# Expert stage of a four-stage kernel: activations laid out with the token innermost, down tables loaded during the up takes, output operations split around the layernorm

## What is computed

```python
def kmoe(x_flat, W_router, A, B, scale, bias, d_in1, d_in2, d_out1, d_out2, top_k):
    logits = x_flat @ W_router.T
    vals, idx = jax.lax.top_k(logits, top_k)
    probs = jax.nn.softmax(vals, axis=-1)
    xs = x_flat.reshape(-1, d_in1, d_in2)
    Ag = A[idx]
    Bg = B[idx]
    Y = jnp.einsum('nkoi,nij,nkpj->nkop', Ag, xs, Bg)
    out = jnp.einsum('nkop,nk->nop', Y, probs).reshape(-1, d_out1 * d_out2)
    return out * scale + bias
...
h = kmoe(x_flat, W_up, A_up, B_up, scale_up, bias_up, D1, D2, F1, F2, TOP_K)      # 32x32 -> 64x64, E=64, TOP_K=2
h = jax.nn.gelu(h, approximate=False)
y = kmoe(h, W_down, A_down, B_down, scale_down, bias_down, F1, F2, D1, D2, TOP_K)  # 64x64 -> 32x32
```

## Time and profile before

| | us |
|---|---|
| median of 3 runs | 875.33 |
| lowest and highest of them | 874.97, 879.26 |
| the profiled execution, its own time | 870.78 |
| its span, first to last instruction | 868.8 |
| granted clock, mean over the span | 0.900 |

### The profile page before, as it was taken

The page is one execution under the profiler, slowest core; times in us unless marked ns, Lnnn a source line. Parts: engine busy times, 40 slices in busy tenths (PEclk is TensorE's granted clock), DMA queues, the critical chain, the costliest instruction groups (busy, mean ns, idle before and its releaser), DMA issues. The chain is left out here.

```text
span 868.8 us, 18294 instructions
## 1 busy us (share of the span) xinstructions
PE 654.9 (75%) x7522; PEld 386.0 (44%) x7554; DVE 519.9 (60%) x1094; ACT 344.7 (40%) x522; POOL 358.8 (41%) x330
## 2 busy tenths in 40 slices
PE   0627878788786389868875478248998988999995
PEld 0313444444444389758765324123333344444442
DVE  8656666676664633221502668878999984415265
ACT  1422444334443653330423463246554535434320
POOL 9202444444442300000001062328998983966530
PEclk9968999999998579878868599659999998999999
DMA  3156540000000632200000470000000000000000
GB/s 76 36 120 150 68 66 0 0 0 0 0 1 1 223 85 49 53 3 2 2 5 5 136 235 0 0 0 1 0 1 0 0 1 1 1 0 1 12 13 24
DMA packets 17326, 29.75 MB, mean 34 GB/s; under 512 B 3248, under 2 KB 13168, under 8 KB 16240
## 3 DMA queue, kind: packets, MB, share of 16 engines
q1 hardware_dynamic: 17264, 28.87, 13.1%
HBM read 24.54 MB, written 4.19 MB: 33 GB/s over the span
## 5 line engine op out<-in xcount | busy, mean ns | idle before, releaser
L474 ACT ACTIVATE pr_exp<-at_psum 128x1024 f32<-128x1024 f32 x68 | 69.6, 1024 | 128.2 <-PE at_psum L559 128.2
L366 DVE TENSOR_REDUCE pr_neg_max<-at_psum 128x4 f32<-128x1024 f32 x68 | 83.2, 1225 | 49.7 <-PE at_psum L541 49.7
L316 POOL TENSOR_SCALAR_AFFINE_SELECT pr_exp<-pr_exp 128x512 f32<-128x512 f32 x68 | 47.1, 692 | 155.6 <-ACT pr_exp L474 155.6
L1481 POOL TENSOR_TENSOR all_phi_b<-all_phi_b,mo_work 128x512 f32<-128x512 f32 x56 | 71.0, 1268 | 44.6 <-ACT mo_work L1687 40.0
L749 POOL TENSOR_TENSOR all_x<-all_x,ff_x_blocks 128x512 f32<-128x512 f32 x3 | 3.8, 1267 | 187.5 <-ACT ff_x_blocks L933 187.5
L1502 PE MATMUL all_psum<-all_phi,mo_xt 128*128 128x512 f32 x128 | 66.3, 645 | 7.4 <-ACT mo_work L1669 5.6
L1451 POOL TENSOR_TENSOR mo_work<-mo_work,mo_max 128x1024 f32<-128x1024 f32 x32 | 61.4, 1918 | 21.5 <-DVE mo_max L1743 21.5
L536 PE MATMUL at_psum<-band_mask,all_ident_bf 128*128 128x512 bf16 x104 | 35.7, 401 | 40.9 <-DVE pr_q_window L359 27.6
L1535 PE MATMUL all_psum<-mo_xt,all_phi_centred 128*128 128x512 f32 x128 | 66.3, 598 | 0.0
L1588 PE MATMUL all_psum<-mo_work,mo_y_slots 128*128 128x512 f32 x128 | 62.5, 595 | 1.8 <-DVE mo_work L1791 1.8
L1687 ACT ACTIVATE mo_work<-all_psum 128x512 f32<-128x512 f32 x64 | 37.7, 601 | 61.9 <-PE all_psum L1535 61.9
(11 more groups left out here) (339 smaller groups left out, 1335.6 us busy)
## 6 DMA issues: line engine op xcount, KB each, us to landing
all_expert_w<-in_expert_w SPq DMA_DIRECT2D x1, 4096.0 KB, 18.2
ff_b_up<-in_b_up SPq DMA_DIRECT2D x1, 2048.0 KB, 9.1
ff_a_up<-in_a_up SPq DMA_DIRECT2D x1, 2048.0 KB, 14.0
ff_w_down<-in_w_down SPq DMA_DIRECT2D x2, 1024.0 KB, 20.7
at_q_stack<-parts_scratch SPq DMA_DIRECT2D x24, 64.0 KB
at_k_stack<-parts_scratch SPq DMA_DIRECT2D x24, 64.0 KB
at_q_stack<-parts_scratch SPq DMA_DIRECT2D x12, 128.0 KB
at_k_stack<-parts_scratch SPq DMA_DIRECT2D x12, 128.0 KB
```

The source lines that it names most:

```text
L316: nc.gpsimd.affine_select(out=e[:, g, :, 0, :], in_=e[:, g, :, 0, :], compare_op=ALU.is_ge, fill=0.0, base=0, pattern=[[0, GH], [-1, P]], ...
L366: nc.vector.tensor_reduce(negm[:, GH * g:GH * g + GH].rearrange("p (u r) -> p r u", r=2), psum[:, SN + 2 * (g % 2):SN + 2 * (g % 2) + 2, : ...
L474: nc.scalar.activation(e[:, g, :, :, :].rearrange("p h j q -> p (h j q)"), psum[:, ST:ST + 2, :].rearrange("p b n -> p (b n)"), ACT.Exp).t ...
L1481: nc.gpsimd.tensor_tensor(tot[:, ch % 2, :], first, ec[:, ch % 2, j, :], ALU.add).then_inc(added, 1)
```

## The change

Four edits, all in `kmoe`. One: `h` becomes `[P, F1, N]`, so that one number of all 128 token positions stands side by side and the 64 numbers of a token position stand 512 bytes apart. L815 then writes single numbers 512 bytes apart, L906 works on 32 runs of 32, the down logits' moving operand (`h[rows, o, :]`) is one run, and the weights of `first_down` (`h[rows, :, n]`) are read 512 bytes apart. Two: `z` and `vs` move to `ta`, the down tables to `tb`. Three: SP waits for 16 instead of 32 take units in front of the down tables' four DMAs. Four: `finish` in `norm_y` is split. VectorE does `variance(gr)`, `take_y(gr+1)`, `invert(gr)`; ScalarE does `root_y(0)`, `take_v(6)`, `norm_y(0)`, `take_v(7)`. Line numbers behind L849 move by up to 5.

```diff
-        h = a.sb("h", [P, N, F1])
+        h = a.sb("h", [P, F1, N])
...
-        z = tb_flat.rearrange("p (u g k n) -> p u g k n", u=2, g=16, k=K)
-        vs = tb_flat.rearrange("p (u s n k b) -> p u s n k b", u=4, s=2, n=8, k=K)
-        bdn = ta_flat[:, 0:D1 * F1].rearrange("p (b n) -> p b n", b=D1)
-        adn = ta_flat[:, D1 * F1:].rearrange("p (b n) -> p b n", b=D1)
+        z = ta_flat.rearrange("p (u g k n) -> p u g k n", u=2, g=16, k=K)
+        vs = ta_flat.rearrange("p (u s n k b) -> p u s n k b", u=4, s=2, n=8, k=K)
+        bdn = tb_flat[:, 0:D1 * F1].rearrange("p (b n) -> p b n", b=D1)
+        adn = tb_flat[:, D1 * F1:].rearrange("p (b n) -> p b n", b=D1)
...
-                sp.wait_ge(got, 2 * UB)
+                sp.wait_ge(got, UB)
...
-                        v.scalar_tensor_tensor(out=h[:, 32 * j + r:32 * j + 32:4, :], in0=psum[:, h_bank(4 * j + r), :].rearrange("p (g o) -> p g o", o=F1),
+                        v.scalar_tensor_tensor(out=h[:, :, 32 * j + r:32 * j + 32:4].rearrange("p o g -> p g o"), in0=psum[:, h_bank(4 * j + r), :].rearrange("p (g o) -> p g o", o=F1),
...
-                    ln_y.finish(dve, 4 * gr, 4 * gr + 4, gr)
+                    ln_y.variance(dve, 4 * gr, 4 * gr + 4)
...
                     norm_y(gr)
                     if gr < 3:
                         take_y(gr + 1)
+                    ln_y.invert(dve, 4 * gr, 4 * gr + 4, gr)
...
-                        part = h[:, 32 * j + 16 * k:32 * j + 16 * k + 16, :].rearrange("p n o -> p (n o)")
+                        part = h[:, 32 * k:32 * k + 32, 32 * j:32 * j + 32]
...
+                def root_y(gr):
+                    ln_y.root(act, 4 * gr, 4 * gr + 4, gr)
+
                 def norm_y(gr):
-                    ln_y.root(act, 4 * gr, 4 * gr + 4, gr)
                     act.wait_ge(ln_y.factors, gr + 1)
...
                 for ch in range(6):
                     take_v(ch)
+                root_y(0)
+                take_v(6)
                 norm_y(0)
-                take_v(6)
                 take_v(7)
                 for gr in range(1, 4):
+                    root_y(gr)
                     norm_y(gr)
...
-                        last = t_.matmul(psum[col:col + 64, s, 0:N], wdn[rows, o, :], h[rows, :, o], start=(o < 2), stop=(o >= F1 - 2))
+                        last = t_.matmul(psum[col:col + 64, s, 0:N], wdn[rows, o, :], h[rows, o, :], start=(o < 2), stop=(o >= F1 - 2))
...
-                                last = t_.matmul(psum[64 * w:64 * w + 64, v_bank(ch) + s, 64 * n2:64 * n2 + 64], h[rows, n, :],
+                                last = t_.matmul(psum[64 * w:64 * w + 64, v_bank(ch) + s, 64 * n2:64 * n2 + 64], h[rows, :, n],
```

More of the change, by code:

```diff
@@ L682, in kmoe @@
         ln, ln_y = Norm(nc, a, "ln_x", NT), Norm(nc, a, "ln_y", NT)
-        flat = h[:, :, :].rearrange("p n o -> p (n o)")
+        flat = h[:, :, :].rearrange("p o n -> p (o n)")
         xt = flat[:, 0:T * R]
```

## The result

Measured again side by side, the kernel before takes 877.59 us (median of 7 runs, 874.97 to 881.57) and the changed kernel 868.26 us (median of 7, 865.43 to 872.73). The ratio is 0.9898, with a 95% interval of 0.9867 to 0.9929: 9 us less, 6 to 12. A second comparison of 5 rounds gives 0.9891 [0.9864, 0.9919]. The direction held, and 868.26 lies inside the range of 855 to 870. The size did not hold: the sum promised 15.1 us, and 868.26 is outside the forecast's own 856 to 864, in the part of rival 1.

What follows compares the result with a forecast made beforehand. The prediction took TensorE to bound the down logits, and instruction supply plus take_y waits the down products. Its terms, -9.9 - 3.7 - 1.5 = -15.1 us from 875.33, gave 860.2 us (forecast 856 to 864, range 855 to 870).

Steps and rivals of the forecast that it cites:

- rival 1: Gain partly eaten: first_down at 56 ns a row removes Term C's gain; 865 us, range 864 to 870, chance 0.22.
- Term A: Down logits: with the moving operand as one run they fall from 18.66 to 8.8 us, gain 9.9.
- Term B: Down products: first_down's strided weight loads take 35 ns a row, hidden by the instruction supply; cost 0.
- L815, the term that failed: Writes of single numbers into h: cost taken as 0, upper bound 0.4 us each, 2.5 us on the path.
- Term C: Down products: reordered output operations remove take_y pauses; supply of 3.45 us a block limits the gain to 3.7 us.
- Rival 4: More than forecast: supply not fixed at 3.45 us a block, reordering gives 6.55; 857 us, chance 0.04 (under 856).
- Term D: Up products, second(0): down table loads 14 us earlier no longer delay an instruction block; gain 1.5 us, between 0 and 3.0.
- The tail: End of the down products: VectorE's last adds are untouched and the tail behind 480.7 stays.
- Rivals 2 and 3: First_down's strided loads don't overlap, 893 us, chance 0.11; repeated PSUM adding, not stride, sets logits' pace, 870, chance 0.08.

Runs made afterwards that it cites:

- logits_run: Kernel before, with the down logits' moving operand read as one run of 128 numbers from the old layout (wrong numbers); 864.23 us in one profiled run.
- after_again: The changed kernel measured once more without edit, 5 rounds; 865.17 us against 874.57 for the kernel before, ratio 0.9891.
- weights_run: Changed kernel, with first_down's weights read as one run of 64 numbers (wrong numbers); 864.24 us in one profiled run.
- layout_only: Kernel before with the new layout of h alone; 872.45 us against 876.43, ratio 0.9954.
- packed_tail: Changed kernel, with each h write going to 8 adjacent token positions and the third group's invert back ahead of the last take_y; 861.89 us, ratio 0.9838.
- order_only: Kernel before with only the output operations reordered; 874.27 us against 876.43, ratio 0.9972.
- half_second: Changed kernel, with only the first expert's half of second_down computed, 512 matmuls and 512 weight loads fewer; 850.96 us in one profiled run.
- loads_only: Kernel before with the down tables loaded 14 us earlier and the buffers swapped; 876.35 us against 876.43, ratio 0.9987.
- tail_order: Changed kernel, with only the third group's invert put back ahead of the last take_y; 863.0 us against 878.11, ratio 0.982.

## Why the prediction was right in sign and two thirds in size

First, the level. Side by side, the kernel before has 877.59 us, 2.3 more than the 875.33 that the forecast started from. The same sum from there gives 862.5, so 5.8 of the 8.1 us between 860.2 and 868.26 are errors of the terms and the rest is this shift.

**Term A, right; one number off.** Forecast 18.66 to 8.8, measured 9.95: 8.7 won instead of 9.9. The pace is L1049's in the windows (some 53 and 27 ns when the whole stage is divided at 398.3), and `logits_run` shows that the step alone made it. What was mis-sized is the moment of the clock's rise. I took 395, 4.2 us into the stage (the trace of before has 394.6); in after the granted clock is 0.50 for 5.7 us, until 398.3. Each microsecond at 0.50 instead of 1.00 costs about half a microsecond now that the rows follow the clock, where the strided rows did not care. That moment varies between executions: the ten profiles with one run have 8.70 to 10.11 us, among them 8.70 in `after_again`, where the forecast's 8.8 is met. The 67 and 70 ns of the prediction are windows divided by rows cut by their edges; from start to start both are 71 ns, which makes its reading, one pace at either clock, only firmer.

**Term B, right, with a condition that I saw only in part.** The middle value of 35 ns came out as 35 to 37, and `weights_run` shows the stage no shorter without it, within the 1.4 us that it varies. The prediction costed B as if C were given. `layout_only` has B without C, and there 1.9 us of `first_down`'s slower rows stand in front of the `take_y` pauses: the order of the terms matters. By medians edit one alone gives 4.0 us, edit four 2.2, edits two and three 0.1; together 6.3, against 9.3 for all four. Each of the three has an interval of 2 to 3 us to either side, so all of the 3 us may be chance; that the slower rows are on the path in `layout_only` rests on its rows, not on the medians.

**L815, the term that failed.** I took 0 and a bound of 0.4 us for each write, from TensorE's penalty for a strided number. Measured is 0.35 us each, near the bound. The writes go in pairs, and two of them took 1.41 us before and 2.05 after. At the three places on the path (j = 0, 1 and 3) the rows of after fall behind those of before by 0.60, 0.63 and 0.58 us, some 1.8 us. As a whole time it was not measured by itself, and `packed_tail`, which takes it back, is only 0.4 us shorter than `after_again` in the up stage, as a stretch there ran at half clock. The wrong step was to take runs of 4 numbers, 256 bytes apart, as the nearest row for single ones. The right bound was in hand and was left out of the sum. The Trainium skill, "SBUF — State Buffer", Door 1: The DMA port swizzle, with its 16-byte lines, had spoken against this write: runs of 4 fill such a line, single numbers don't, and the three rows (746 ns for runs of 8, 1122 for steps of 16 bytes, 1100 for 512) agree with it.

**Term C, the mechanism right, the size not.** The pauses went, and the supply was what came next, as the prediction said. It took 3.45 us for a block from one clean step of the earlier trace rows, and so 41.65 us would become 37.95. From fetch to fetch, twelve steps take 43.56 us in after, 3.63 each, 44.75 in `after_again`, 3.73 each, and 46.30 in `packed_tail`, 3.86 each; single ones go up to 4.00 in `order_only` and from 3.35 to 4.13 in `half_second`. So the stage is 1.6 us shorter than before's in after, 0.6 in `order_only`, 0.2 in `after_again` and longer in `packed_tail`: C's size lies between nothing and 1.6 us in these executions, not at 3.7, and it is not firmer known than that. The kernel before had four steps of 3.43 to 3.46 us in a row, where `logits_run`, with the same code in that stretch, has 3.70 to 4.01, and the lowest step of a supply is no mean of it. Rival 4, that the supply gives way and C brings 6.55, is excluded: `order_only` has all `take_y` waits removed and still takes 45.30 us, `weights_run` 44.47. Why one step is 3.4 us and another 4.1 is open; no run changed it by itself. The granted clock does not part them: before has 3.45 at 0.50, and `half_second` has both 3.35 and 4.13 at 1.00. The transfer of a block is not the whole step either: 1.9% of 16 engines over 48 us, for 13 blocks, is 1.1 us each.

**Term D, a wash.** The pause in second(0) fell by 1.3 us (forecast 1.5), and 0.45 us came back at the end of the takes, where the loads had been moved. I had counted 3.3 us of cover there. With L815's 1.8 us, 85 matmuls that took 1.1 us less, and three block steps in second(2) and second(3) that are longer by 0.75 us together, the up stage ends where it did, +0.2 us. `loads_only` could not be told from the kernel before.

**The tail, missed.** "VectorE's last adds are untouched" was wrong. The order of VectorE's last instructions is the same, but `invert(2)` stands behind `take_y(3)`, so the scaling of group 2, and with it GpSimd's addition, starts later and lands on VectorE's L84. 0.87 us, given back by `tail_order`; `order_only` and `weights_run` show the addition at 1.03 and 1.04 us too, with tails of 14.15 and 14.16. In after it ends at 476.97, just behind GpSimd's, which ends at 476.95. The Trainium skill, "SBUF — State Buffer", Who interferes with whom, says that a VectorE instruction with two SBUF inputs contends with a GpSimd instruction that reads SBUF; the 1.03 and 0.17 us agree. In `after_again` GpSimd's addition starts 0.13 us behind L84's, which takes 0.17; there L88, with one input, takes 1.12 us instead of 0.17 and ends with GpSimd's at 474.3, so it is not this addition alone that is held.

**The account.** Forecast -15.1. A +1.2, C +2.1, L815 +1.8, D's smaller gain, the new pause and the longer block steps +1.4, the tail +0.9: that is 7.4 less, -7.7, against -9.0 in the stages. Of the rest, 1.1 us is one row of the up stage: the 85 matmuls behind the pause took 1.50 us in after and 2.61 in the earlier trace rows. `loads_only`, `after_again` and `packed_tail`, with 2.62, have it as before, so I count it as chance. This account is of one execution. In `after_again` the sum is the same, -9.1, but A is at its forecast and C brings 0.2 us, so the shares of A and C are in part luck of the profile, while L815's and the tail's recur in every profile that has them. Rival 1, the gain partly eaten, is the case that came about, though not by its own main step (56 ns a row) but by L815's bound and by C's smaller gain. Rivals 2 and 3 are excluded by rows: 37 ns where 77 decides, and 9.38 us.

## What to carry to other kernels

When an operand's layout is turned for one reader, price every other reader and writer of it at its own innermost run: runs of 8 numbers were free here and single ones cost half as much again, and a permutation inside the layout gave both sides what they want. A stage of small f32 products can be bound by the number of its instructions; then slower rows are free, but only as long as no other wait stands behind them, and removed waits bring only what the supply's mean pace allows, not its best step. Take the pace and the price of a stage from more than one execution: here one kernel's stages differed by up to 1.4 us between two. When an operation is pulled ahead of another on one engine, look also at what the delayed one starts on a third engine, and what that will overlap.

## What the runs showed of the hardware

- In the down products TensorE was supplied with 256 instructions in 3.35 to 4.13 us, about 14 ns for each load or matmul; taking 1024 away took 14.6 us, 7.4 of busy time and 7.1 of pauses. The steps did not follow the granted clock.
- A moving operand of 128 f32 numbers costs 71 ns a row from start to start when they stand 256 bytes apart, at either clock, and 53 or 27 ns in one run.
- Weight loads of 64 columns 512 bytes apart to four quadrants go by at 35 to 37 ns a row, at either clock, against 112 ns estimated from the earlier trace rows for one alone: they overlap.
- VectorE takes 1100 ns to write 512 single f32 numbers a partition 512 bytes apart, 1122 ns at 16 bytes, 746 ns in runs of 8, with PSUM read 256 bytes apart in the last two.
- Bulk loads of 2 MB in one go delayed the next block of instructions at a place with an estimated 3.3 us of cover: 0.17 to 0.59 us of pause in eight profiles, none with the loads spread. At second(0) the pause was 3.04 to 3.54 us behind such loads and 1.22 to 1.78 without.
- A VectorE addition of 4 numbers a partition took 1.03 us beside a GpSimd addition of 512, and 0.17 alone; a VectorE operation with one input of the same size took 1.12 us beside it.
